# Moving the conversion of the output weights within an attention kernel: twelve early heads two units later, twenty late heads at other steps, three more of them on POOL, and one activation table load ahead

## The reference, cut to what matters

```python
x = x + einsum('bct,bcd->bdt', x, weights[subjects])
q, k, v = x @ Wq.T, x @ Wk.T, x @ Wv.T           # 32 q heads, 8 k and v heads of 128
q, k = rope(rmsnorm(q, q_norm_w)), rope(rmsnorm(k, k_norm_w))
kc, vc = k_cache[block_table], v_cache[block_table]   # 16 pages of 32 tokens, masked by length
scores = einsum('bqhd,bkhd->bhqk', q, concat(kc, k)) * SCALE
probs = softmax(where(valid, scores, -1e30))
o = einsum('bhqk,bkhd->bqhd', probs, concat(vc, v)).reshape(b, s, 32 * 128)
x = x + einsum('bse,de->bsd', o, Wo)
```

## Time and profile before

| | us |
|---|---|
| median of 3 runs | 1014.4 (1013.04 to 1017.41) |
| the profiled execution, whole | 1013.84 |
| its span | 1012.0 |
| PE busy | 967.1 (96%) |
| DVE busy | 818.9 (81%) |
| ACT busy | 736.2 (73%) |
| POOL busy | 539.9 (53%) |

### The profile page before, as it was taken

How to read it: one execution, slowest core, us unless ns; L and a number is a source line. 1 busy time by engine, 2 the same in 40 slices (tenths; PEclk the granted TensorE clock), 3 DMA queues, 4 the chain that set the end, 5 groups by cost and what they waited for, 6 DMA issues and landing times.

```text
span 1012.0 us, 24821 instructions
## 1 busy us (share of the span) xinstructions
PE 967.1 (96%) x8123; PEld 802.1 (79%) x8123; DVE 818.9 (81%) x1752; ACT 736.2 (73%) x2007; POOL 539.9 (53%) x709
## 2 busy tenths in 40 slices
PE   6899999999889988899999999999999999989998
PEld 4678888887678777778788888888888888878885
DVE  7889999999997698878878777777787787777770
ACT  5898999988775687767767676676776676766660
POOL 5565665566882167546554554455545544544440
PEclk9999999999999999999999999999999999999999
DMA  5799999989989889999999999989998998999940
GB/s 196 289 314 336 326 390 362 387 277 392 387 319 308 315 308 337 347 240 264 275 305 259 279 313 284 296 274 285 313 259 279 306 300 248 318 290 277 262 125 11
DMA packets 249904, 294.89 MB, mean 291 GB/s; under 512 B 79025, under 2 KB 206513, under 8 KB 247217
## 3 DMA queue, kind: packets, MB, share of 16 engines
q1 hardware_dynamic: 231088, 226.07, 75.0%
q0 software_dynamic: 18688, 67.25, 17.7%
HBM read 231.77 MB, written 46.27 MB: 275 GB/s over the span
## 4 chain that ended last, share of the span: by engine, by line
PE 65%; DVE 15%; issue 6%; ACT 6%; POOL 4%; DMA 3%; SPq 1%; DVEq 0%; ACTq 0%; POOLq 0%
PE ps_y L1489 15%; PE ps_o L1564 13%; PE ps_proj L1489 12%; PE ps_s L1527 7%; PE ps_s L1531 6%; PE ps_t L1538 6%; DVE rot L1361 2%; PE ps_rt L1659 2%; DVE probs L1228 2%; DVE stage L1371 1%; DVE rot L1353 1%; DVE c_stage L1385 1%; PE ps_t L1546 1%; ACT probs L1008 1%; PE ps_o L1576 1%
## 5 line engine op out<-in xcount | busy, mean ns | idle before, releaser
L934 POOL TENSOR_SCALAR probs<-probs,recip 128x544 f32<-128x544 f32 (+1 forms) x256 | 161.5, 631 | 298.3 <-DVE recip L1236 291.3
L1008 ACT ACTIVATE probs<-probs,neg_max 128x544 f32<-128x544 f32 x256 | 190.9, 746 | 150.8 <-DVE neg_max L1228 147.2
L1228 DVE CUSTOM_DVE_ANT_0 probs<-ps_s,mask,row_scale 128x544 f32<-128x544 f32 x256 | 200.5, 783 | 68.0 <-PE ps_s L1531 64.7
L1564 PE MATMUL ps_o<-pt,vs 128*128 128x128 f16 x3072 | 213.3, 219 | 1.9 <-DMA vs<-v_pages,v_row 1.9
L1564 PEld LDWEIGHTS ps_o<-pt,vs 128*128 128x128 f16 x3072 | 192.7, 98 | 16.5 <-DMA vs<-v_pages,v_row 2.4
L887 POOL TENSOR_TENSOR roped<-rot 128x256 f32<-128x256 f32 x160 | 145.2, 929 | 80.8 <-DVE rot L1353 77.6
L1248 DVE SCALAR_TENSOR_TENSOR pt<-ps_t,pt 128x512 f16<-128x512 f32 x190 | 130.0, 684 | 49.0 <-ACT pt L1014 48.9
L1489 PE MATMUL ps_proj<-wt_hi,x0t_hi 128*128 128x512 f32 x384 | 159.0, 415 | 5.9 <-DVE x0t_lo L1186 5.7
L1489 PE MATMUL ps_y<-wo,ot_hi 128*128 128x512 f16 x512 | 153.5, 381 | 2.6 <-DVE ot_lo L1260 2.6
L1489 PE MATMUL ps_proj<-wt_hi,x0t_lo 128*128 128x512 f32 x384 | 150.7, 394 | 0.0
L1489 PE MATMUL ps_proj<-wt_lo,x0t_hi 128*128 128x512 f32 x384 | 149.8, 391 | 0.0
(11 more groups left out here) (155 smaller groups left out, 1653.4 us busy)
## 6 DMA issues: line engine op xcount, KB each, us to landing
kt<-k_pages_t SPq DMA_DIRECT2D x512, 128.0 KB
c_nat<-in_L_cond_k_cache SPq DMA_DIRECT2D x32, 512.0 KB, 6.0
q_t<-stage SPq DMA_DIRECT2D x64, 256.0 KB, 7.3
c_nat<-in_L_cond_v_cache SPq DMA_DIRECT2D x32, 512.0 KB, 6.6
qt<-q_t SPq DMA_DIRECT2D x32, 512.0 KB, 3.7
w_nat<-in_L_cond_Wq SPq DMA_DIRECT2D x8, 1024.0 KB, 7.9
k_pages_t<-c_stage SPq DMA_DIRECT2D x16, 512.0 KB, 5.1
c_nat<-in_L_cond_Wo SPq DMA_DIRECT2D x16, 512.0 KB, 7.4
```

What stands on the lines that cost most here:

```text
L934: pool.tensor_scalar(part, part, col(recip, i), 1.0, ALU.mult, ALU.mult).then_inc(p_norm, 1)
L1008: act.activation(pr, pr, ACT.Exp, bias=col(neg_max, i), scale=-1.0, accum_out=col(row_sum, i)).then_inc(a_exp, 1)
L1228: dve.tensor_tensor_reduce(out=probs_of(i), in0=ps_s[:, score_cols(i):score_cols(i) + KEYS], in1=mask[(i // HK) % 2][:, mask_at(i):mask_at ...
L1564: ins = pe.matmul(ps_o[n % 2][:, jl * P:(jl + 1) * P], v[:, part, :], pt[pt_slot(i)][:, NCH * half + c, :], start=jl == 1 and c == 0 and k ...
```

## The change

- The twelve early heads are converted in units 89 to 94 instead of 87 to 92.
- The twenty late heads are converted at the steps `WO_LATE` = 4, 8, 12, 16, 20, 22, 24, 27, 29, 32, 34, 36, 39, 41, 44, 46, 48, 51, 53, 56 instead of 1, 4, 7, ..., 58.
- A low half goes to POOL where its step (one behind the high half) has i % 8 of 1 or 7, steps on which POOL issues no gather. These are steps 9, 17, 23, 25, 33, 47, 49 and 57: eight heads on POOL instead of five, twelve on DVE in phase 2 instead of fifteen.
- In unit 92 ACT makes an exponential of one column that nobody reads. The load of the table of exponentials, which stood between the masks and the first exponential, is thereby made in unit 92.

```diff
-    WO_EARLY, WO_EARLY_AT = 12, 87
+    WO_EARLY, WO_EARLY_AT = 12, 89
+    WO_LATE = (4, 8, 12, 16, *(20 + 12 * k // 5 for k in range(HQ - WO_EARLY - 4)))
@@
     def late_head(i):
 
-        k, r = divmod(i, 3)
-        return WO_EARLY + k if i >= 0 and r == 1 and WO_EARLY + k < HQ else None
+        return WO_EARLY + WO_LATE.index(i) if i in WO_LATE else None
 
     def on_pool(n):
-        return n >= WO_EARLY and n % 4 == 3
+        return n >= WO_EARLY and (WO_LATE[n - WO_EARLY] + 1) % HK in (1, HK - 1)
 
     def by_pool(n):
 
-        return max(0, n - WO_EARLY) // 4
+        return sum(on_pool(m) for m in range(n))
@@ the scalar engine's program, phase 1
                 for n in early_heads(u):
                     wo_high(n)
+                if u == SCORES_AT - 1:
+                    act.activation(norm_sums[:, 1:2], minus_one[:], ACT.Exp)
                 if u == SCORES_AT:
```

## The result

| | before | after |
|---|---|---|
| median | 1014.4 us (1013.04 to 1017.41, 7 runs) | 1012.13 us (1010.4 to 1012.32, 7 runs) |
| the profiled execution, whole | 1013.84 | 1012.16 |
| its span | 1012.0 | 1010.1 |

The ratio over all runs is 0.9969, with a 95% interval of 0.9954 to 0.9983: 3.1 us (the two medians lie 2.3 apart), less than the 0.5% that tell a change from none. A second set of runs, both kernels on one chip, gave 1015.44 (13 runs) and 1010.74 us (4), 0.9949 (0.9933 to 0.9966), which is 5.2 us and stands on that line.

What follows compares the result with a forecast made beforehand. PE, busy for 96% of the span, was taken as the bound, so only its idle time could be won. Terms summed to 4.9 us off 1013.84, with the median 0.56 above, rounded to 1009.4 us; range 1005.5 to 1014.

Steps and rivals of the forecast that it cites:

- The start: Start of the attention loop: 0.7 us later, 0.5 won back by the head off step 1; 0.2 lost in all.
- Step 10: Steps 7 to 10: DVE's maximum comes earlier without head 14 ahead of it; 0.9 us won, bounds 0 and 0.96.
- Steps 11 to 18: Head 15's low half leaves POOL, where it delays norms PE awaits; 2.2 us won, bounds 1.0 and 2.65.
- The wait for values at step 19: PE's 1.62 us wait for gathered values shrinks; 0.3 us won, bounds 3.1 lost and 1.6 won.
- Steps 24 to 31: Covered by the term for steps 17 to 31: one low half fewer on DVE, 0.2 us won, bounds 0 and 1.5.
- Steps 32 to 58: Eleven heads instead of nine, under longer PE steps with room on DVE and ACT: zero, 0.5 us either way.
- Steps 59 to 63: Head 31's half on POOL moves to step 57, ending waits at 62 and 63; 1.7 us won, bounds 1.2 and 1.75.
- The sum: Whole kernel: all terms together, 4.9 us won against the profiled execution of 1013.84 us.
- Transfers: Rival: the gain comes back as waits for transfers, at step 19; 1.5 us won, 1012.9 us, chance 0.22.
- More is won: Rival: unflagged small gaps and the last wait for values go too; 8.1 us won, 1006.3 us, chance 0.18.
- POOL's free steps are not free: Rival: POOL halves in steps without gathers cost up to 1.85 us each; 1015.4 or 6.6 us lost, 1021; chance 0.07.
- The preload isn't one: Rival: the table goes back for a mask or copy, two more loads at the start; 1011.5 us, chance 0.05.

Runs made afterwards that it cites:

- late_only: The changed kernel with its early heads back in units 87 to 92 and the table loaded in unit 93: 1010.24 us, ratio 0.9944.
- before_again: The kernel before, unchanged, profiled once more: 1016.47 us in its one run.
- start_88: The changed kernel with early heads in units 88 to 93 and the table loaded in unit 84: 1009.88 us, ratio 0.9926.
- spread_up: start_88 with only five late heads below step 32 and fifteen from 32 to 56, POOL's halves at five steps: 1012.23 us, ratio 0.9973.
- two_to_dve: The kernel before with the low halves of heads 15 and 31 on DVE instead of POOL, all steps kept: 1012.18 us, ratio 0.9945.
- after_again: The changed kernel, unchanged, profiled once more: 3.5 us below before_again from the first scores to the end.
- later_24: The changed kernel with the heads of steps 24, 27, 29 at 25, 28, 31, and head 22's low half on POOL instead of head 21's: 1012.69 us, one run.
- tuned: start_88 with late heads re-placed (25 and 28 for 24, 27, 29; others moved from 35 on), eight halves on POOL: 1009.45 us, ratio 0.9933.
- no_preload: The changed kernel without the one-column exponential in unit 92: 1011.69 us, one run.
- two_gathers: start_88 with two more gathers of the first values on POOL in phase 1, each waited for: 1016.04 us, ratio 1.0011.

## Why the prediction was right, and where it was not

The time, 1012.13, lies in the range and within 0.5% of before, the case given the most chance (0.54). It is 2.7 us above the forecast of 1009.4, and part of the agreement is luck (below). Step by step, with the ledger of after (and late_only, before_again where they help):

- **The start.** Predicted +0.7, then -0.5 for head 12 off step 1, in all 0.2 lost. Measured +0.64 at scores 3 and +0.12 at scores 8. The maxima were to start at 344.1 and 348.4; they start at 346.51 and 350.78, which less the 2.44 us of phase 1 is 344.07 and 348.34. The norm of step 4 takes 0.72 instead of 1.25. What failed is a side of it: "Worth to PE by itself: nothing", of the wait for heads 8 to 11. ACT and DVE do not catch up by unit 93: what the wait has above 2.47 us is felt one for one, and start_88, with 0.53 of it left and no pair in unit 94, starts 1.28 us ahead of before. What a wait between 0.53 and 2.47 costs, no run shows. The sum came out because the replay was made against a trace with a wait of 3.25; in other executions of the same code the start is up to 0.8 earlier by luck of the load, and in after it stands at +0.65 each time.
- **Step 10.** Predicted 0.9 won; 0.87 (scores 8 to 14). The earlier trace rows had the cause.
- **Steps 11 to 18.** Predicted 2.2 won, with 0.2 lost for three POOL halves in free steps. Measured 1.35 won from 14 to 22. The head at step 8, with its half on POOL at 9, costs 0.51 between the scores of 14 and 15, behind the gap of 0.30 at 376.01 (start_88 goes from -2.49 to -1.97, spread_up, with no head at step 8, stays at -2.49); by 22 it is 0.37, and spread_up, without it, wins 1.72. So the 0.2 for three was too small, and 2.2 was too large by 0.5. The price of 2.65 for head 15 was too high: taken off POOL alone it brought 0.87 (two_to_dve), since on DVE it costs too.
- **The wait for values at step 19.** Predicted 0.3 won, with 1.0 to 1.6 left. It was 0.58 in after and 0.92 in after_again, less than that, and 22 to 24 gave 1.17 in after and 0.12 in after_again, where the wait for keys at step 21 took 0.55 back. The bounds of the gain held; the term is not one number but varies by about 1 us, and the sum had no term for the keys.
- **Steps 24 to 31.** Here the sum is wrong. "Steps 17 to 31: gain 0.2, bounds 0 and 1.5", worked out from the count of low halves on DVE. Measured: 1.76 lost from 28 to 34, outside the bounds, and 1.06 won from 34 to 42, where before had losses of its own. I counted heads on DVE and did not replay ACT's queue at the new steps, where step 24's mask, the new keys' copy of step 28 and the split of rows stand. later_24 and tuned show that it is the place of these heads: both are free of the loss between 28 and 34. Which of the three costs what, no run shows.
- **Steps 32 to 58.** Predicted 0 within 0.5; 0.19 lost from 42 to 64. It holds for these eleven heads; the fifteen of spread_up lose 4.45.
- **Steps 59 to 63.** Predicted 1.7 won; 1.99 (64 to 67).
- **The sum.** 4.9 predicted, 4.57 by the ledger of after and 3.50 by that of after_again. In the first, 0.9 us more than forecast at steps 19 to 21 makes up by luck for what steps 11 to 18 and 24 to 42 fell short of (0.34 lost between the scores of 24 and 42, against 0.2 forecast as won). The executions of after with the higher mean clock took 1010.4 to 1010.55, 1.1 above the forecast; the other 1.6 us of the distance go with a lower mean granted clock (below), which no term of the sum had.

**The rivals.** *Transfers* came in a small part: the wait at step 19 fell, but in after_again 0.55 us came back as a wait for keys at step 21. *More is won* was right in its idea, as tuned shows (7.6 us), and wrong of this change. *POOL's free steps are not free* had a part, 0.51 at step 9; but the largest gap behind a norm from there to 516 us is 0.55, at 382.53, far from the 1.6 a head at which it would decide. *The preload isn't one* fell: behind the preload no table load follows in after, and it is worth 0.39.

## What to carry to other kernels

When work is moved to other places of an in-order queue, replay every engine that takes it at the new place, with all that the place already has (here a mask, a copy of the new keys, a split of rows), and don't sum counts. Look first at the one helper engine whose queue leads to the bound through a long operation (here a gather, then a norm): two heads taken off it gave most of what moving twenty did. And look for the waits for transfers that stand next in line: they took part of the gain back in some executions and not in others. Buffers of the bound engine don't hide a long wait of a helper when, a unit or two later, the same helper makes what the bound engine waits for.

## What the runs showed of the hardware

**The granted clock of TensorE falls behind short idle times, in some executions.** Each execution has PE idle for 2.8 us at about 28 us, and for 2.36 us at step 222. What follows differs between executions of programs that are the same there. Stretches of no_preload, before and after (the same code until unit 87; columns of the earlier trace rows, the clock third from the end):

```profile
28.00:50.50 22.50, 20.53 (x99) 15.54 (x100) 20.20 (x32) 19.92 (x69) 12.91 (x24) 1.00 0.86 297
```

```profile
28.00:50.50 22.50, 20.34 (x89) 15.29 (x90) 18.67 (x30) 18.36 (x64) 12.04 (x21) 0.92 0.80 288
```

```profile
28.00:50.50 22.50, 20.94 (x86) 15.66 (x86) 17.43 (x28) 17.19 (x58) 11.63 (x21) 0.86 0.75 273
```

By these means the clock was at half (1.2 GHz) for about 0, 3.6 and 6.3 us, an estimate from the rows. PE's products at about 46 us stand 1.77 earlier in no_preload than in before and 1.01 later in after. The first scores come at 339.84, 340.52 and 342.96 us. So the clock is about 1.0 of the 2.44 us that made the profiled execution of after look worse than it is. Some 0.4 more arise near 90 us, and 1.0 at about 270, where the clock is 1.00 and PE waits for DVE longer than in before. First before, then after:

```profile
269.35 0.63 PE L1659 MATMUL ps_rt<-fixed,roped 128*128 128x128 f32 x4 [0.57 <-DVE stage L1371]
```

```profile
271.39 0.63 PE L1661 MATMUL ps_rt<-fixed,roped 128*128 128x128 f32 x4 [1.06 <-DVE stage L1373]
...
272.35 0.51 PE L1491 MATMUL ps_proj<-wt_hi,x0t_hi 128*128 128x512 f32 x1 [0.34 <-DVE wt_lo L1198]
```

Eleven of the fourteen profiles lose this 1.0 us; before, later_24 and tuned do not. Its cause stays open. At step 222 the timelines of PE, of before and then of before_again:

```profile
905.37 0.65 PE L1538 MATMUL ps_t<-fixed,probs 128*128 128x128 f32 x4 [2.36 <-POOL probs L934]
```

```profile
906.59 1.12 PE L1538 MATMUL ps_t<-fixed,probs 128*128 128x128 f32 x4 [2.36 <-POOL probs L934]
```

and the 2.5 us from there on, by stretch, in the same order:

```profile
905.40:907.90 2.50, 2.50 (x33) 2.37 (x34) 0.95 (x2) 0.60 (x1) 2.22 (x3) 1.00 0.89 305
```

```profile
906.60:909.10 2.50, 2.50 (x18) 2.40 (x19) 0.69 (x1) 0.60 (x1) 2.19 (x3) 0.50 0.90 292
```

Behind the same gap one goes on at 1.00 (2.4 GHz) and the other at 0.50 (1.2 GHz), with 18 matmuls instead of 33 in 2.5 us and 1.12 us instead of 0.65 for the same transposes. It costs 1.2 to 1.7 us (the ledger from 224 to 240, as -3.43 to -1.88 in after_again) and occurs in 8 of the 14 profiles; the idle time before it is 2.35 or 2.36 in all. The times of one kernel go with the mean granted clock of the execution in most cases, though not in all: two_to_dve took 1009.94 us at 1.000, 1012.17 and 1012.19 at 0.998 and 1014.54 at 0.995; after took 1010.4 to 1010.55 at 0.998 and 0.999 and 1012.13 to 1012.32 at 0.996 and 0.997. In spread_up 1015.05 us, its longest, stands at 0.997 and 1013.94 at 0.994: other things vary as well, such as the waits for transfers and the one near 270 us. Two executions of one kernel so lie up to 5.9 us apart (two_gathers, 1013.17 and 1019.04), more than the change is worth.

**The gap at step 222 itself** stands behind a gather that POOL issues 2.8 us late, in all fourteen profiles. From the timeline of POOL in after:

```profile
901.07 1.34 POOL L922 DMA_INDIRECT vs<-v_pages,v_row  x1 [2.84 <-PE ps_o L1566]
902.48 0.72 POOL L934 TENSOR_SCALAR probs<-probs,recip 128x544 f32<-128x544 f32 x1
```

It does not move with the count of gathers (two_gathers). The releaser that the trace names, a product of PE, does not tell why it is this step and no other. The cause stays open.
